# Statistics arithmetic moved to ScalarE, the first block by halves, and an earlier store of the reciprocals, in a linear-attention kernel

## The reference, cut to what matters

```
# group norm: 32 groups of 8 channels over all tokens, eps 1e-5, no affine part
xn = (x - mean) / sqrt(var + eps)
q, k, v = split(xn.T @ qkv_w.T + qkv_b)        # 6400 x 256 each
q = relu(q);  k = relu(k + pos_enc)            # 8 heads of 32 channels
z  = 1 / (q . sum_tokens(k) + 1e-6)            # per head and token
kv = k.T @ v                                   # per head, 32 x 32
out = (q @ kv) * z                             # no softmax
y = x + (out @ proj_w.T + proj_b)
```

## Time and profile before

| what | value |
|---|---|
| median of 3 runs | 2663.91 us |
| the profiled execution | 2665.23 us, of which the trace's span is 2663.4 us |
| granted TensorE clock, mean over the span | 0.998 |
| busy: PE, POOL, ACT, DVE | 2593.6, 1974.8, 1661.0, 1603.5 us |
| ended the chain of work: PE, DVE, issue, ACT, POOL, DMA | 80, 6, 5, 4, 3, 2 % |
| HBM traffic | 639 MB, 240 GB/s over the span |

### The profile page before, as it was taken

The page is one execution under the profiler, slowest core; times in us unless marked ns, Lnnn a source line. Parts: engine busy times, 40 slices in busy tenths (PEclk is TensorE's granted clock), DMA queues, the critical chain, the costliest instruction groups (busy, mean ns, idle before and its releaser), DMA issues.

```text
span 2663.4 us, 44657 instructions
## 1 busy us (share of the span) xinstructions
PE 2593.6 (97%) x15812; PEld 2214.4 (83%) x15812; DVE 1603.5 (60%) x2500; ACT 1661.0 (62%) x2544; POOL 1974.8 (74%) x1218
## 2 busy tenths in 40 slices
PE   4989999999999999999999999999999999999998
PEld 4878888788888888888888888888878888788886
DVE  6655656566665565656656555566666666555547
ACT  4656666566666656656566666656656566665664
POOL 5958777687786868768687786877768678686875
PEclk9999999999999999999999999999999999999999
DMA  7557867677776767767677677776868777675668
GB/s 257 185 171 240 274 219 260 221 258 248 240 262 230 267 221 256 265 225 251 229 251 263 229 262 250 253 256 217 263 217 267 237 249 257 211 256 192 229 208 296
DMA packets 323163, 641.99 MB, mean 241 GB/s; under 512 B 24704, under 2 KB 46080, under 8 KB 322944
## 3 DMA queue, kind: packets, MB, share of 16 engines
q1 hardware_dynamic: 322944, 639.14, 71.5%
HBM read 519.25 MB, written 119.80 MB: 240 GB/s over the span
## 4 chain that ended last, share of the span: by engine, by line
PE 80%; DVE 6%; issue 5%; ACT 4%; POOL 3%; DMA 2%; ACTq 0%; SPq 0%; DVEq 0%; POOLq 0%
PE banks L582 18%; PE banks L606 17%; PE banks L639 16%; PE banks L594 12%; PE banks L596 6%; PE banks L573 5%; PE banks L624 4%; ACT xn L1051 2%; DVE kk L875 1%; DVE stats L853 1%; DVE banks L870 1%; POOL hl L1253 1%; ACT kk L1073 1%; POOL kacc L1267 1%; ACT xt L1068 1%
## 5 line engine op out<-in xcount | busy, mean ns | idle before, releaser
L1267 POOL TENSOR_TENSOR kacc<-kacc,kt 128x512 f32<-128x512 f32 x368 | 477.4, 1297 | 330.8 <-ACT kt L1080 328.6
L582 PE MATMUL banks<-wqk,hl 128*128 128x256 f32 x4608 | 646.4, 290 | 12.8 <-POOL hl L1253 12.8
L1253 POOL TENSOR_TENSOR hl<-xn,hl 128x512 fp32r<-128x512 f32 x384 | 493.9, 1309 | 213.1 <-ACT hl L1063 212.9
L859 DVE TENSOR_TENSOR xt<-banks,xt 128x512 fp32r<-128x512 f32 x400 | 274.5, 686 | 567.6 <-ACT xt L1068 567.5
L606 PE MATMUL banks<-hl,wqk 128*128 128x512 f32 x2304 | 601.2, 396 | 12.9 <-DVE xr L889 12.9
L582 PEld LDWEIGHTS banks<-wqk,hl 128*128 128x128 f32 x4608 | 576.0, 191 | 17.7 <-POOL hl L1253 17.7
L594 PE MATMUL banks<-kk,xt 128*128 128x512 f32 x1600 | 584.5, 399 | 4.1 <-DVE kk L875 4.1
L639 PE MATMUL banks<-uhl,mhl 128*128 128x512 f32 (+1 forms) x2316 | 542.4, 383 | 2.1 <-DVE xr L889 2.1
L639 PEld LDWEIGHTS banks<-uhl,mhl 128*128 128x128 f32 x2316 | 424.2, 188 | 89.8 <-issue 2.5
L606 PEld LDWEIGHTS banks<-hl,wqk 128*128 128x128 f32 x2304 | 406.0, 188 | 108.1 <-DVE xr L889 17.1
L1287 POOL TENSOR_TENSOR q<-q,zb 128x1024 f32<-128x1024 f32 x180 | 433.7, 2409 | 78.0 <-DMA zb<-z_rows 77.8
(11 more groups left out here) (117 smaller groups left out, 2406.8 us busy)
## 6 DMA issues: line engine op xcount, KB each, us to landing
posb<-pos_plus_bk SPq DMA_DIRECT2D x375, 256.0 KB, 4.9
xs<-in_x SPq DMA_DIRECT2D x184, 512.0 KB, 6.8
xa<-in_x SPq DMA_DIRECT2D x184, 512.0 KB, 6.1
xr<-in_x SPq DMA_DIRECT2D x184, 512.0 KB, 3.9
zb<-z_rows SPq DMA_DIRECT2D x184, 512.0 KB, 6.0
y<-xr SPq DMA_DIRECT2D x184, 512.0 KB, 7.1
z_rows<-zt SPq DMA_DIRECT2D x32, 256.0 KB, 5.4
xr<-in_pos SPq DMA_DIRECT2D x25, 256.0 KB, 5.1
```

The lines of the kernel that those rows point to most:

```text
L582: last = mm(psK[:, par(n, h), i * C:(i + 1) * C], hl_of(t)[:, a, c, s:s + P], wqk[:, w, c, C:2 * C], start=(j == 0), stop=(j == len(terms) ...
L1253: g.tensor_tensor(hl_of(t)[:, 1, :, s], xn_of(n, t)[:, :, s], hl_of(t)[:, 0, :, s], ALU.subtract).then_inc(xl_ready, 1)
L1267: g.tensor_tensor(both, both, kt[:, par(n, h), :], ALU.add).then_inc(ks_done, 1)
```

## The change

- The small arithmetic of the statistics is split anew. DVE keeps what reads PSUM (four instructions for the two averages) and the reciprocal. ACT takes the rest with its scale and bias operands, one channel column per instruction: `gn_square` (two instructions) at t = 10 behind `u_step`, for which PE's L565 now waits, and `gn_rstd` (four dependent pairs) at t = 11 behind `u_step` and ahead of `key_high` of half 23. In image 0 both stand at the end of ACT's steps 10 and 11. DVE's reciprocal moves ahead of the residual of step 11.
- POOL makes the low part of the next image's block 0 ahead of the key sum of half 24.
- At the start ACT copies the weights' high part before its root, block 0 is normalised and split by halves, DVE adds the first position rows in POOL's place, the wait for the weights' low part moves behind PE's first transposes, and PE multiplies zeros 5, 2 and 6 times around the two averages.
- SP stores the reciprocals of the first 8 blocks sooner in step 1. The load that spreads them stays where it was.
- `m_total` writes its sum back into its PSUM bank, and the two splits read it there (not for the last image). `g_copy` therefore waits for less, and the first output's second bank for more.

The diff, cut to its core:

```diff
--- before.py
+++ after.py
@@ -471,6 +479,8 @@
                         load_last(i)
+                if t == 1 and not first(n):
+                    store_z(n - 1, 0)
...
@@ -486,7 +496,6 @@
                 if t == 1 and not first(n):
-                    store_z(n - 1, 0)
...
@@ -557,16 +566,19 @@
                     pe.wait_ge(setup_done, 1)
-                pe.wait_ge(gn_step, 10 * n + 1)
+                pe.wait_ge(gn_step, 4 * n + 1)
...
             def gn_group_var(n):
-                pe.wait_ge(gn_step, 10 * n + 4)
+                pe.wait_ge(gn_spread, n + 1)
...
                 t, tok = h // 2, h % 2 * HALF
-                pe.wait_ge(xh_ready, blk_no(n, t))
+                if first(n) and h == 0:
+                    pe.wait_ge(xh_first, 1)
+                else:
+                    pe.wait_ge(xh_ready, blk_no(n, t))
...
@@ -574,6 +586,8 @@
                 pe.wait_ge(xl_ready, half_no(n, h))
+                if first(n) and h == 0:
+                    pe.wait_ge(w_low, 1)
...
@@ -689,15 +703,16 @@
                     elif ot == 0:
-                        pe.wait_ge(m_sum, on + 1)
...
+                        pe.wait_ge(ml_ready, on + 1)
...
                         elif ot == 7 and on + 2 < B:
-                            pe.wait_ge(gn_step, 10 * (on + 2) + 2)
+                            pe.wait_ge(gn_step, 4 * (on + 2) + 2)
                         elif ot == 8 and on + 2 < B:
-                            pe.wait_ge(gn_step, 10 * (on + 2) + 5)
+                            pe.wait_ge(gn_step, 4 * (on + 2) + 3)
...
@@ -795,10 +810,19 @@
+            def keep_running(k):
...
+                for _ in range(k):
+                    mm(psK[:, 1, 0:C], kvm[:, 0, :], kvm[:].rearrange("p c n -> p (c n)"), start=True, stop=True)
...
+            pe.wait_ge(warm_ready, 1)
+            pe.wait_ge(first_stats, NBLK - 3)
+            keep_running(5)
             gn_group_mean(0)
+            keep_running(2)
             gn_group_var(0)
+            keep_running(6)
             pe.wait_ge(w_loaded, 16 * 5)
-            pe.wait_ge(w_low, 1)
...
@@ -817,37 +841,24 @@
                 dve.wait_ge(gn_mean, n + 1)
-                dve.wait_ge(gn_step, 10 * n + 1)
-                v.tensor_copy(gmean[:], psX[:, 1, 0:CC])
+                dve.wait_ge(gn_step, 4 * n + 1)
...
+                v.tensor_scalar(gmean[:], psX[:, 1, 0:CC], -1.0, None, ALU.mult)
                 v.tensor_tensor(gdev[:], mv[:, :, 0], psX[:, 1, 0:CC], ALU.subtract).then_inc(gn_step, 1)
-                dve.wait_ge(gn_step, 10 * n + 2)
-                v.tensor_tensor(gtmp[:], gdev[:], gdev[:], ALU.mult).then_inc(gn_step, 1)
-                dve.wait_ge(gn_step, 10 * n + 3)
-                v.tensor_tensor(gvar[:], gtmp[:], mv[:, :, 1], ALU.add).then_inc(gn_step, 1)
...
                 dve.wait_ge(gn_var, n + 1)
-                v.tensor_scalar(gvar[:], psX[:, 1, 0:CC], GN_EPS, None, ALU.add).then_inc(gn_step, 1)
...
-            def gn_rstd(n):
+                v.tensor_scalar(gvar[:], psX[:, 1, 0:CC], GN_EPS, None, ALU.add)
+                v.tensor_scalar(gdev[:], psX[:, 1, 0:CC], GN_EPS, -0.5, ALU.add, ALU.mult).then_inc(gn_step, 1)
...
+            def gn_inverse(n):
...
                 v.reciprocal(grs[:], gtmp[:]).then_inc(gn_step, 1)
-                dve.wait_ge(gn_step, 10 * n + 6)
-                v.tensor_tensor(gdev[:], grs[:], grs[:], ALU.mult).then_inc(gn_step, 1)
-                dve.wait_ge(gn_step, 10 * n + 7)
-                v.tensor_tensor(gdev[:], gdev[:], gvar[:], ALU.mult).then_inc(gn_step, 1)
-                dve.wait_ge(gn_step, 10 * n + 8)
-                v.tensor_scalar(gdev[:], gdev[:], -0.5, 1.5, ALU.mult, ALU.add).then_inc(gn_step, 1)
-                dve.wait_ge(gn_step, 10 * n + 9)
-                wait(dve, xn_ready, NBLK * n)
-                v.tensor_tensor(rstd[:], grs[:], gdev[:], ALU.mult).then_inc(gn_step, 1)
-                dve.wait_ge(gn_step, 10 * n + 10)
-                v.scalar_tensor_tensor(out=nbias[:], in0=gmean[:], scalar=-1.0, in1=rstd[:],
-                                       op0=ALU.mult, op1=ALU.mult).then_inc(gn_ready, 1)
...
                 if t == 0:
-                    dve.wait_ge(gn_step, 10 * (n - 1) + 1)
+                    dve.wait_ge(gn_step, 4 * (n - 1) + 1)
...
@@ -909,17 +920,17 @@
-            def m_total(n, bank):
+            def m_total(n, bank, total):
...
                 for c in range(CC):
-                    last = v.scalar_tensor_tensor(out=mt[:, c, :], in0=bpb[:, c, :], scalar=ksc[:, c:c + 1],
+                    last = v.scalar_tensor_tensor(out=total[:, c, :], in0=bpb[:, c, :], scalar=ksc[:, c:c + 1],
...
-            def m_low(n):
+            def m_low(n, total):
...
                 mw = mhl_last if n == B - 1 else mhl
-                v.tensor_tensor(mw[:, 1, :, :], mt[:], mw[:, 0, :, :], ALU.subtract).then_inc(ml_ready, 1)
+                v.tensor_tensor(mw[:, 1, :, :], total, mw[:, 0, :, :], ALU.subtract).then_inc(ml_ready, 1)
...
@@ -935,12 +946,14 @@
                     g_total(n - 1)
+                if t == 11 and n + 1 < B:
+                    gn_inverse(n + 1)
...
@@ -952,7 +965,7 @@
                     if t == 2 and junction:
-                        m_low(n - 1)
+                        m_low(n - 1, in_bank(psX[:, 1]))
...
@@ -1010,8 +1021,15 @@
             v.memset(zeps, Z_EPS)
-            v.memset(kvm[:], 0.0)
+            v.memset(halves3, 1.5)
+            v.memset(kvm[:], 0.0).then_inc(warm_ready, 1)
...
+            def pos_first(h):
...
+                dve.wait_ge(raw_landed[h], 16)
+                v.tensor_tensor(by_part(posb[:, h, :]), by_head(pos_raw[:, h, :]),
+                                by_head(bk_b[:].rearrange("p i n -> p (i n)")), ALU.add).then_inc(pos_added, 1)
...
@@ -1024,7 +1042,8 @@
             gn_variance(0)
-            gn_rstd(0)
+            gn_inverse(0)
+            pos_first(0)
...
@@ -1033,9 +1052,37 @@
+            def gn_square(n):
...
+                act.wait_ge(gn_step, 4 * n + 2)
+                for c in range(CC):
+                    last = a(gvar[:, c:c + 1], gdev[:, c:c + 1], ACT.Identity, bias=mv[:, c, 1:2], scale=gdev[:, c:c + 1])
+                last.then_inc(gn_spread, 1)
...
             def gn_root(n):
-                act.wait_ge(gn_step, 10 * n + 5)
+                act.wait_ge(gn_step, 4 * n + 3)
...
+            def gn_rstd(n):
...
+                def each(out, src, scale, bias, done):
+                    for c in range(CC):
+                        k = slice(c, c + 1)
+                        if bias is None:
+                            last = a(out[:, k], src[:, k], ACT.Identity, scale=scale[:, k])
+                        else:
+                            last = a(out[:, k], src[:, k], ACT.Identity, bias=bias, scale=scale[:, k])
+                    last.then_inc(done, 1)
...
+                act.wait_ge(gn_step, 4 * n + 4)
+                each(gtmp, grs, gdev, None, gn_newton)
+                act.wait_ge(gn_newton, 3 * n + 1)
+                each(gvar, gtmp, grs, halves3, gn_newton)
+                act.wait_ge(gn_newton, 3 * n + 2)
+                wait(act, xn_ready, NBLK * n)
+                each(rstd, gvar, grs, None, gn_newton)
+                act.wait_ge(gn_newton, 3 * n + 3)
+                each(nbias, gmean, rstd, None, gn_ready)
...
@@ -1103,7 +1150,7 @@
-                wait(act, ml_ready, n)
+                wait(act, kv_done, n)
...
@@ -1140,7 +1187,10 @@
                 if t == 10:
+                    gn_square(1)
                     gn_root(1)
+                if t == 11:
+                    gn_rstd(1)
...
@@ -1165,11 +1215,15 @@
                     u_step(n, t)
+                if t == 10 and n + 1 < B:
+                    gn_square(n + 1)
+                if t == 11 and n + 1 < B:
+                    gn_rstd(n + 1)
...
@@ -1231,13 +1285,24 @@
-            gn_root(0)
+            gn_square(0)
...
             last.then_inc(w_high, 1)
-            normalise(0, 0)
-            xn_high(0, 0)
+            gn_root(0)
+            gn_rstd(0)
+            act.wait_ge(gn_ready, 1)
+            for h in halves(0):
...
+                k = slice(h * HALF, (h + 1) * HALF)
+                for c in range(CC):
+                    last = a(xn_of(0, 0)[:, c, k], q_of(0, 0)[:, c, k], ACT.Identity,
+                             bias=nbias[:, c:c + 1], scale=rstd[:, c:c + 1])
+                last.then_inc(xn_half if h == 0 else xn_ready, 1)
+                act.wait_ge(xn_half if h == 0 else xn_ready, 1)
+                high = a(hl_of(0)[:, 0, :, k], xn_of(0, 0)[:, :, k], ACT.Copy)
+                high.then_inc(xh_first if h == 0 else xh_ready, 1)
...
@@ -1301,13 +1366,14 @@
                     scale(*u_of(n, t))
+                if t == LAST and n + 1 < B:
...
+                    xn_low(n + 1, 0)
...
                     xn_low(n, t + 1)
-                elif n + 1 < B:
-                    xn_low(n + 1, 0)
...
@@ -1321,8 +1387,16 @@
```

(11 more changed lines are left out.)

25 lines of the change are left out of this document (15 added, 10 removed).

## The result

The changed kernel takes 2635.94 us (median of 4 runs, 2635.40 to 2637.06) against 2663.07 us for the kernel before on the same chip: a ratio of 0.9903, with a 95% interval of 0.9885 to 0.9920. The profiled execution took 2637.06 us (span 2635.3) against 2665.23. The forecast was 2641, in a range of 2632 to 2656; 28.2 us went where it counted 22.7. Two executions behind the experiments, one of e9 (4296 us) and one of the kernel before (3656 us), ran at a mean granted clock of 0.56 and 0.66 and are left out of every comparison.

A forecast was written before the change was run, and what follows sets the result against it. PE, busy 97% of the span, gains only where it stands still. From the profiled 2665.23 us, -21.3 + 1.8 + 1.4 - 0.8 - 3.3 - 0.5 = -22.7 gave 2642.5; forecast median 2641, range 2632 to 2656.

The forecast's parts named there:

- Rival D: Ends of images: the hold moves to DVE's larger instructions, the wait stays, only image 0 pays; 2660 us, chance 0.06.
- a stall is worth 2.13 us: Ends of ten images: a stalled image takes 163.32 us against 161.19 unstalled; removing ten stalls returns 21.3 us.
- ragged restart: After a stalled image's end: counted with the 1.29 and 0.54 us waits in the 2.13 us a stall costs.
- the 0.81 us wait of the earlier trace: One image, POOL's first scaling: the earlier store of the reciprocals removes this one wait, counted as 0.8 us gained.
- The chain's length: Step 11, gn_rstd on ACT: four dependent pairs take 2.3 us, with ends of 1.3 and 4.2 us.
- rival C: Step 11: gn_rstd ahead of half 23's keys becomes a wait in every image; 2685 us at a 4.2 us chain, chance 0.05.
- The remainder of 0.13 us at step 12: Ends of images: normalise starts at 310.5, latest free start 310.37, so 0.13 us stays in 14 images, 1.8 us lost.
- The second average: Step 10: PE's second average waits for ACT's gn_square pair, 0.1 us in each of 14 images, 1.4 us lost.
- -3.5 forecast: End of image 0: idle falls from 3.17 to 1.2 us and the clock stays up; with +0.2 at step 10, -3.3.
- the 0.5 us of gain: The start: key add 1.25 us sooner at full clock, 0.5 us gain taken; bounds 2.5 gained, 1 lost.
- the drain: The start: the Trainium skill adds about 1.38 us per table switch; with it the start would lose 0.9 us.
- The ten stalls: Ends of images: ten images counted as stalled in the profiled execution, returning 21.3 us in all.

The follow-up runs named there:

- e9: The changed kernel with gn_rstd's chain on DVE right behind the reciprocal, both columns per instruction and two SBUF inputs: 2635.61 us, ratio 0.9909.
- e1: The changed kernel with the statistics arithmetic back on DVE in its old places: 2648.58 us, ratio 0.9936.
- e2: The changed kernel with POOL's key sum of half 24 again ahead of the next image's low part: 2650.09 us, ratio 0.9945.
- e3: The kernel before with only the statistics chain moved to ACT; start, POOL and SP as before: 2652.74 us, ratio 0.9955.
- e11: The kernel before with only POOL's low part of the next image's block 0 ahead of the key sum: 2648.61 us, ratio 0.9951.
- e6: The changed kernel with ACT's gn_rstd chain run twice in step 11: 2669.84 us, ratio 1.0032.
- e8: The changed kernel with gn_rstd's chain on DVE, one column per instruction with a per-partition scalar, ahead of the residual: 2634.91 us, ratio 0.9904.
- e12: The changed kernel unchanged, run again beside other experiments on the same chip: 2635.64 us, ratio 0.9909.
- e5: The changed kernel without the 13 zero products at the start: 2635.42 us, ratio 0.9904.

## Why the prediction was right, point by point

**The two causes.** It held that the stall of an image's end comes from `gn_rstd` on DVE and from POOL's order. Both are shown, each by being put back (e1, e2) and by being done alone (e3, e11). Rival D, the hold moving to the larger DVE instructions, is out: no wait for the residual is left at an image's end. (The images that ran without a stall were four, not the three it names.) That a stall is worth 2.13 us held as well: PE's lead grows by 2.37 us in a stalled image and by 0.24 in another. The "ragged restart" in it is mostly the second wait of 0.54 us and the stretch ahead of it that the list does not count (e2). Up to the mark at 2432.34 there are ten waits of 1.29 us and nine restarts of 0.84 behind them, 20.5 us; the 0.81 us wait of the earlier trace rows is gone as charged; 3.5 of the 24.83 us are left, and they are the missing term below.

**The chain's length.** 2.3 us forecast, 2.19 measured. The prices for one and two operands, 0.29 and 0.375 us, are 0.283 to 0.287 and 0.379 in the trace. This was what decided between forecast and rival C, and e6 shows that C's mechanism is real. C's price for e6's chain of 4.43 us would be 1.65 x (4.43 - 2.14) = 3.78 us an image; 1.97 were measured. PE waits 1.15 + 0.34 = 1.49 us instead of 2.29, since the cover was thicker than thought (below), and each us of wait cost 1.32, not 1.65. (C sets its price against 25.7 us gained elsewhere; its own terms add up to 21.3 + 0.8 + 3.3 + 0.5 = 25.9.)

**The terms that were mis-sized** are small ones, all in the same direction:

- *The remainder of 0.13 us at step 12, 1.8 us.* It was 0. The term rested on 0.4 us of cover for key half 23 and on a normalise at 310.5, 2.77 us behind the k product of half 24. Measured are 1.07 us of cover and 2.08. ACT stands earlier against PE at the end of the image, which the working took from the rows of before as if it were fixed. In step 10 its copy of u starts 2.08 us behind PE's k product instead of 2.67, and in step 11 ACT is free for the chain 2.95 us ahead of the k product of half 24 instead of 2.65; the keys then start 2.10 us behind the chain's start, not 2.3. The change itself moved ACT, by taking the square and the sum of step 9 off DVE. The prediction priced them only by image 0's wait, but beside POOL they were held too (before, image 1; POOL's instructions end at 284.38 and 285.62):

```profile
283.38 1.01 DVE L824 TENSOR_TENSOR gtmp<-gdev 128x2 f32<-128x2 f32 x1
284.43 1.21 DVE L826 TENSOR_TENSOR gvar<-gtmp,mv 128x2 f32<-128x2 f32 x1
```

  The kernels sort by this. Where these two are on DVE (before, e1, e11), ACT's normalise of step 10 starts 0.37 us ahead of PE's k product in most images. Where they are ACT's (the changed kernel, e2, e3, e8, e9), it starts 1.39 us ahead (0.97 in image 1 of the changed kernel). In most earlier steps its place is the same in both. No run moves the square and the sum alone.
- *The second average, 1.4 us.* Also 0, for the same reason: the pair ended 0.6 us before PE wanted it.
- *A term that was missing, 3.5 us.* Images without a stall lost 0.25 us each as well. PE's distance from transpose (642.82) to k product (643.41) was 0.59 us in such an image before, and is 0.36 after: POOL's low part, then still behind the key sum, came that much late, and since PE's transposes were still running no idle time is listed. e11 shows it by itself: with the order alone such an image takes 160.94 us. The working took an unstalled image as one with no wait, and so left POOL's order without a value there.

Together 6.7 us. The tenth restart, 0.8 us, was not gained: from the mark to the end both kernels take 231.1 us. That leaves the 5.9 us between 24.83 and 18.9. By the k products PE's lead is 29.1 us at 2434.98 and still at the last of them, in image 15. It falls to 28.2 in the last outputs, where PE waits 0.32 us for the residual at 2608.84 and 0.30 at 2617.66, neither of which the kernel before has; ahead of the second DVE had waited 0.61 us for a load of x. The second execution of the changed kernel (e12) has neither wait and is 0.7 us shorter behind the last k product, so it need not be the change's.

**Image 0.** -3.5 forecast, -3.92 measured at its end, and the clock did not fall after 0.69 us of idle. The second average's wait was said to be 1.45 us and is 1.56, and PE's wait of 1.25 us for DVE at 134.96, on the other side of the trade, is gone. The trade cost 0.40 us instead of 0.2.

**The start.** The term that failed is the 0.5 us of gain: +0.16 was measured. The first k product was forecast at 33.2 and came at 33.54, and at 33.24 in e12. The gain that hung on the clock did not come: 0.53 was granted at the first k product, and what the first two won in other executions was lost at the wait for POOL ahead of the third (e5: 0.07 us in all). The table load was on the path in full, as forecast; the drain was not there.

**Luck.** The ten stalls were counted from one execution, and the number changes from one to the next. With the eight of e11 the same sum would have been 2 x 2.13 = 4.3 us smaller. It fitted because the measured traces compare with that same execution.

**Not tested.** No run puts m back in SBUF alone, or undoes the start by halves alone. e11's period of 160.94 us without the change to m leaves nothing for it in an image.

## What to carry to other kernels

When an instruction of a few elements takes microseconds, look at what the neighbouring engine runs and where that ends: if both end together, change the instruction's form or place before moving the work to another engine. A kernel whose runs spread over 17 us, beside one that spreads over 2, can be a sign of it. An iteration without a visible wait is not free of waits: compare the distances between the same two instructions in the best and in the changed case. And price a wait by the period, not by its own length, since 0.28 us of it cost 0.55. When a small chain moves, look also at what its old place delayed further on.
